# Second MoE of a two-layer block: slots gather rows of x from DRAM by an inverse permutation made on the chip and store their sums straight to the output

## The reference, cut to what matters

```python
def _L1_ffn_ref(hidden_states, router_w, gate_w, up_w, down_w):
    x = hidden_states.reshape(-1, hidden_shape[-1])
    route = jax.nn.sigmoid(x @ router_w)
    max_ind = jnp.argmax(route, axis=1)
    max_prob = jnp.take_along_axis(route, max_ind[:, None], axis=1)
    out = jnp.zeros_like(x)
    for e in range(num_experts):
        mask = (max_ind == e)[:, None]
        h = jax.nn.silu(x @ gate_w[e]) * (x @ up_w[e])
        out = out + jnp.where(mask, h @ down_w[e], 0.0)
    out = out * max_prob
    return out.reshape(hidden_shape)
...
x = x + _L1_xattn_ref(_layernorm(x, axis=-1), ctx_2048, mask_BxS2_bk0)
x = x + _L1_ffn_ref(_layernorm(x, axis=-1), L1_ffn_router_w, L1_ffn_gate_w, L1_ffn_up_w, L1_ffn_down_w)
```

## Time and profile before

| what | us |
|---|---|
| runs shown (3) | 3142.78 to 3145.83, median 3144.97 |
| the profiled execution's own time | 3145.72 |
| its span, first to last instruction | 3143.9 |
| PE, DVE, ACT, POOL busy | 2881.0, 2166.2, 2036.6, 1594.0 |
| granted TensorE clock, mean | 0.964 |

### The profile page before, as it was taken

The page is one execution under the profiler, slowest core; times in us unless marked ns, Lnnn a source line. Parts: engine busy times, 40 slices in busy tenths (PEclk is TensorE's granted clock), DMA queues, the critical chain, the costliest instruction groups (busy, mean ns, idle before and its releaser), DMA issues. The chain is left out here.

```text
span 3143.9 us, 61785 instructions
## 1 busy us (share of the span) xinstructions
PE 2881.0 (92%) x18699; PEld 2447.6 (78%) x18700; DVE 2166.2 (69%) x4564; ACT 2036.6 (65%) x5192; POOL 1594.0 (51%) x2073
## 2 busy tenths in 40 slices
PE   6886999899999999999999999999999977699495
PEld 4665888688888888888888888888888854488363
DVE  7995444577777777777777777777777768766232
ACT  5664666577777777777777777777777557565121
POOL 6993333355555555555555555555555344564201
PEclk9998999899999999999999999999999979899598
DMA  4335666611111111111101101101100020442512
GB/s 134 117 115 172 202 205 204 205 48 40 45 46 49 37 45 52 40 39 52 46 33 52 46 33 52 45 33 52 46 33 33 11 74 1 137 148 65 194 45 79
DMA packets 253176, 244.07 MB, mean 78 GB/s; under 512 B 11768, under 2 KB 233472, under 8 KB 252928
## 3 DMA queue, kind: packets, MB, share of 16 engines
q1 hardware_dynamic: 237248, 223.15, 21.7%
q10 hardware_dynamic: 14144, 13.63, 1.5%
q0 software_dynamic: 1536, 4.20, 0.4%
HBM read 151.03 MB, written 89.92 MB: 77 GB/s over the span
## 5 line engine op out<-in xcount | busy, mean ns | idle before, releaser
L911 ACT ACTIVATE pt_hi<-ps_t 128x512 fp32r<-128x512 f32 (+2 forms) x1024 | 569.9, 557 | 415.2 <-PE ps_t L1156 411.8
L983 DVE TENSOR_REDUCE piece_max<-ps_s 128x1 f32<-128x512 f32 (+2 forms) x1024 | 631.5, 622 | 258.7 <-PE ps_s L1143 231.0
L1009 DVE TENSOR_TENSOR pt_lo<-ps_t,pt_hi 128x512 fp32r<-128x512 f32 (+2 forms) x1024 | 656.3, 641 | 200.3 <-ACT pt_hi L911 183.9
L1083 POOL TENSOR_SCALAR prob<-prob,inv_sum 128x512 f32<-128x512 f32 (+2 forms) x1024 | 636.6, 641 | 270.9 <-DVE inv_sum L999 270.9
L899 ACT ACTIVATE prob<-ps_s,neg_max 128x512 f32<-128x512 f32 (+2 forms) x1024 | 648.8, 634 | 89.3 <-DVE neg_max L990 72.3
L1176 PE MATMUL ps_o<-pt_hi,v_hi 128*128 128x256 f32 (+1 forms) x1856 | 595.8, 321 | 0.0
L1156 PE MATMUL ps_t<-ident,prob 128*128 128x128 f32 (+1 forms) x3712 | 572.1, 272 | 1.4 <-DVE pt_lo L1009 1.3
L1178 PE MATMUL ps_o<-pt_hi,v_lo 128*128 128x256 f32 (+1 forms) x1856 | 523.6, 282 | 0.0
L1177 PE MATMUL ps_o<-pt_lo,v_hi 128*128 128x256 f32 (+1 forms) x1856 | 522.3, 281 | 0.0
L1156 PEld LDWEIGHTS ps_t<-ident,prob 128*128 128x128 f32 (+1 forms) x3712 | 456.7, 140 | 59.8 <-issue 1.7
L1138 PE MATMUL ps_s<-k_hi,q_hi 128*128 128x512 f32 (+2 forms) x1024 | 404.3, 395 | 34.8 <-ACT prob L899 19.8
(11 more groups left out here) (247 smaller groups left out, 5579.5 us busy)
## 6 DMA issues: line engine op xcount, KB each, us to landing
v_scratch<-v_out SPq DMA_DIRECT2D x120, 256.0 KB, 2.5
raw_k<-k_scratch SPq DMA_DIRECT2D x32, 960.0 KB, 5.5
raw_v<-v_scratch SPq DMA_DIRECT2D x32, 960.0 KB, 4.7
k_scratch<-k_out SPq DMA_DIRECT2D x104, 256.0 KB, 2.6
q_scratch<-out_t SPq DMA_DIRECT2D x64, 256.0 KB, 2.6
raw_q<-q_scratch SPq DMA_DIRECT2D x32, 512.0 KB, 3.4
c_raw<-in_ctx_t ACTq DMA_DIRECT2D x52, 256.0 KB, 2.8
raw_t<-in_ctx_t SPq DMA_DIRECT2D x24, 512.0 KB, 4.0
```

The lines of the kernel that those rows point to most:

```text
L911: nc.scalar.activation(pt_hi[keys, k % RING, cols], ps_t[keys, k % 2, cols], ACT.Copy).then_inc(hi_done, 1)
L983: nc.vector.tensor_reduce(piece_max[:, n % 2, p:p + 1], ps_s[:, p, lo - p * PC:hi - p * PC], AX.X, ALU.max).then_inc(max_ready, 1)
L1009: nc.vector.tensor_tensor(pt_lo[keys, k % RING, cols], ps_t[keys, k % 2, cols], pt_hi[keys, k % RING, cols].bitcast(F32), ALU.subtract).th ...
L1083: nc.gpsimd.tensor_scalar(prob[:, n % PB, lo:hi], prob[:, n % PB, lo:hi], inv_sum[:, n % PB:n % PB + 1], 1.0, ALU.mult, ALU.mult).then_inc ...
```

## The change

It keeps no sorted copy of xn and no y in DRAM. ACT stores each tile of x to `x_rows` in DRAM during memory_attention, two tiles behind. The routing takes each token's slot and lane from `place` and makes the inverse permutation by matmuls: `in_lane` (is this token's lane n?) turned against `facts` (token number, mean, rstd and probability, in the column of the token's slot), which leaves in `fact` for each lane and slot the token's four numbers, and from them the row to read and the row to write; a lane with no token reads row 0 and writes beyond the output, where the bounds check drops it. A slot gathers its rows of x by an indirect DMA on POOL, into a ring of four; DVE normalises them, and at the end multiplies y by the probability, adds the gathered x (`finish`) and POOL stores the sum to the output rows. The loops over slots are written out in full. The diff, its declarations and the arguments that only carry names left out; in `turn_x`, `hidden`, `output` only names, waits and the loops change, and ACT's copy of y goes:

```diff
-                sp.wait_ge(zeros_ready, 1)
-                sp.dma_start(sorted_dram.rearrange("(s p) d -> p s d", p=P), zeros[:, :].unsqueeze(1).to_broadcast([P, ESLOTS, D])).then_inc(zeroed, 16)
-                sp.wait_ge(zeroed, 16)
-                nc.gpsimd.memset(zeros[:, :], 0.0).then_inc(zeros_ready, 1)
...
+                def store_rows(i, u):
+
+                    at = i * UB + u
+                    act.wait_ge(x_added, at + 1)
+                    act.sem_inc(store_begun, 1)
+                    act.dma_start(x_rows[bass.ds(at * P, P), :], x_sb[:, bass.ds(at, 1), :].rearrange("p a n -> p (a n)")).then_inc(rows_written, 16)
...
+                            if s == 3 and u >= 2:
+                                store_rows(i, u - 2)
+                            elif s == 3 and positive(i):
+                                store_rows(i - 1, u + 2)
...
+                for u in range(2, UB):
+                    store_rows(LAST, u)
...
+                dve.wait_ge(tokens_made, 1)
+                for n, src in enumerate((token[:, :], mean_var[:, :, 0], rstd[:, :])):
+                    nc.vector.tensor_copy(own[:, :, n], src).then_inc(own_set, 1)
...
-                nc.vector.tensor_copy(max_prob[:, :], best[:, :, 0]).then_inc(prob_copied, 1)
+                nc.vector.tensor_copy(own[:, :, 3], best[:, :, 0]).then_inc(own_set, 1)
...
-                nc.vector.tensor_reduce(place_f[:, :], own_row[:, :, :], AX.X, ALU.add).then_inc(places, 1)
+                nc.vector.tensor_reduce(place[:, :], own_row[:, :, :], AX.X, ALU.add).then_inc(places, 1)
+
                 dve.wait_ge(places, 1)
-                nc.vector.tensor_copy(place[:, :], place_f[:, :]).then_inc(place_ready, 1)
+                nc.vector.tensor_scalar(slot_part[:, :], place[:, :], 1.0 / P, (P - 1) / (2 * P), ALU.mult, ALU.subtract).then_inc(slot_parts, 1)
+                dve.wait_ge(slot_parts, 1)
+                nc.vector.tensor_scalar(slot_int[:, :], slot_part[:, :], TO_INT, None, ALU.add).then_inc(slot_rounded, 1)
+                dve.wait_ge(slot_rounded, 1)
+                nc.vector.tensor_scalar(slot[:, :], slot_int[:, :], TO_INT, None, ALU.subtract).then_inc(slot_ready, 1)
+                dve.wait_ge(slot_ready, 1)
+                nc.vector.scalar_tensor_tensor(lane[:, :], slot[:, :], -float(P), place[:, :], ALU.mult, ALU.add).then_inc(lanes, 1)
+                nc.vector.tensor_tensor(in_slot[:, :, :], iota[:, 0:ESLOTS].unsqueeze(1).to_broadcast([P, NT, ESLOTS]),
+                                        slot[:, :].unsqueeze(2).to_broadcast([P, NT, ESLOTS]), ALU.is_equal).then_inc(in_slots, 1)
+                dve.wait_ge(in_slots, 1)
+                dve.wait_ge(own_set, FACTS)
+                nc.vector.tensor_tensor(facts[:, :, :, :], in_slot[:, :, :].unsqueeze(2).to_broadcast([P, NT, FACTS, ESLOTS]),
+                                        own[:, :, :].unsqueeze(3).to_broadcast([P, NT, FACTS, ESLOTS]), ALU.mult).then_inc(facts_ready, 1)
+                dve.wait_ge(lanes, 1)
+                for part in range(NORM_PARTS):
+                    tiles = slice(part * NORM_TILES, (part + 1) * NORM_TILES)
+                    nc.vector.tensor_tensor(in_lane[:, tiles, :], iota[:, :].unsqueeze(1).to_broadcast([P, NORM_TILES, P]),
+                                            lane[:, tiles].unsqueeze(2).to_broadcast([P, NORM_TILES, P]), ALU.is_equal).then_inc(in_lanes, 1)
 
...
+
+                dve.wait_ge(held, 1)
+                nc.vector.tensor_copy(fact[:, :, :], ps_f[:, :].rearrange("p (n s) -> p n s", n=FACTS)).then_inc(fact_ready, 1)
+                dve.wait_ge(fact_ready, 1)
+                nc.vector.tensor_scalar(read_at[:, :], fact[:, 0, :], 1.0, 0.0, ALU.subtract, ALU.max).then_inc(at_ready, 1)
+                nc.vector.tensor_scalar(beyond[:, :], fact[:, 0, :], 0.0, float(2 * TOK), ALU.is_equal, ALU.mult).then_inc(beyond_ready, 1)
+                dve.wait_ge(beyond_ready, 1)
+                nc.vector.tensor_tensor(holds[:, :], beyond[:, :], fact[:, 0, :], ALU.add).then_inc(holds_ready, 1)
+                dve.wait_ge(holds_ready, 1)
+                nc.vector.tensor_scalar(write_at[:, :], holds[:, :], 1.0, None, ALU.subtract).then_inc(at_ready, 1)
                 dve.wait_ge(table_ready, 1)
-                dve.wait_ge(prob_copied, 1)
+                dve.wait_ge(at_ready, 2)
...
+                pe.wait_ge(facts_ready, 1)
+                for t in range(NT):
+                    if t % NORM_TILES == 0:
+                        pe.wait_ge(in_lanes, t // NORM_TILES + 1)
+                    last = nc.tensor.matmul(ps_f[:, :], in_lane[:, t, :], facts[:, t, :, :].rearrange("p n s -> p (n s)"), start=t == 0, stop=t == NT - 1)
+                last.then_inc(held, 1)
...
+                nc.gpsimd.iota(token[:, :], [[P, NT]], base=1, channel_multiplier=1, allow_small_or_imprecise_dtypes=True).then_inc(tokens_made, 1)
                 for part in range(NORM_PARTS):
                     norm_rstd(nc, pool, mean_var, rstd, half, norm, part)
-                pool.wait_ge(xn_ready, NT)
-                pool.wait_ge(place_ready, 1)
-                for t in range(NT):
-                    nc.gpsimd.indirect_dma_start(sorted_dram, bass.IndirectOffsetOnAxis(ap=place[:, t:t + 1], axis=0), xn[:, t, :], None).then_inc(scattered, 16)
-                pool.wait_ge(scattered, 16 * NT)
...
+    RING = 4
+    LEAD = RING
-        xs = sb("xs7", [P, 2, D])
+        xg = sb("xg7", [P, RING, D])
+        xn = sb("xn7", [P, 2, D])
-        y = sb("y7", [P, 2, D])
-        back = sb("back7", [P, NT, D])
+        made = sb("made7", [P, RING, D])
...
-                def load(s, j, n):
-
-                    if positive(n):
-                        sp.wait_ge(xt_ready, s - 1)
-                        sp.sem_inc(io_begun, 1)
-                    sp.dma_start(xs[:, j, :], sorted_dram[bass.ds(s * P, P), :]).then_inc(xs_loaded[j], 16)
-
-                def step(s, j):
-                    if exists(s + 3):
-                        load(s + 3, 1 - j, 1)
-                    sp.wait_ge(y_copied, s + 1)
-                    sp.sem_inc(io_begun, 1)
-                    sp.dma_start(y_dram[bass.ds(s * P, P), :], y[:, j, :]).then_inc(y_written[j], 16)
-
-                load(0, 0, 0)
-                load(1, 1, 0)
-                load(2, 0, 1)
-                all_slots(sp, step)
-                for q in range(4):
-                    sp.wait_ge(x_added, (q + 1) * Q)
-                    sp.dma_start(out_dram[:, q * Q:(q + 1) * Q, :], x_sb[:, q * Q:(q + 1) * Q, :]).then_inc(out_written, 16)
-                sp.wait_ge(out_written, 16 * 4)
...
+            @block.gpsimd
+            def _(pool):
+                def gather(s):
+                    nc.gpsimd.indirect_dma_start(xg[:, s % RING, :], None, x_rows,
+                                                 bass.IndirectOffsetOnAxis(ap=read_at[:, s:s + 1], axis=0)).then_inc(gathered[s % RING], 16)
+
+                pool.wait_ge(rows_written[0], rows_written[1])
+                for s in range(LEAD):
+                    gather(s)
+                for s in range(ESLOTS):
+                    pool.wait_ge(made_ready, s + 1)
+                    nc.gpsimd.indirect_dma_start(out_rows, bass.IndirectOffsetOnAxis(ap=write_at[:, s:s + 1], axis=0), made[:, s % RING, :], None,
+                                                 bounds_check=TOK - 1, oob_is_err=False).then_inc(written[s % RING], 16)
+                    if s + LEAD < ESLOTS:
+                        gather(s + LEAD)
+                for j in range(RING):
+                    pool.wait_ge(written[j], 16 * ((ESLOTS + RING - 1 - j) // RING))
...
-                    act.wait_ge(y_done, s + 1)
-                    if positive(s - 1):
-                        act.wait_ge(y_written[j], 16 * (s // 2))
-                        act.sem_inc(io_begun, 1)
-                    nc.scalar.activation(y[:, j, :], ps_y[:, j, 0:D], ACT.Copy).then_inc(y_copied, 1)
...
+                def normalise(s):
+                    dve.wait_ge(gathered[s % RING], 16 * (s // RING + 1))
+                    if s >= 2:
+                        dve.wait_ge(xt_ready, s - 1)
+                    nc.vector.tensor_scalar(xn[:, s % 2, :], xg[:, s % RING, :], fact[:, 1, s:s + 1], fact[:, 2, s:s + 1],
+                                            ALU.subtract, ALU.mult).then_inc(xn_ready, 1)
+
+                def finish(s):
+
+                    dve.wait_ge(y_done, s + 1)
+                    if s >= RING:
+                        dve.wait_ge(written[s % RING], 16 * (s // RING))
+                    nc.vector.scalar_tensor_tensor(made[:, s % RING, :], ps_y[:, s % 2, 0:D], fact[:, 3, s:s + 1], xg[:, s % RING, :],
+                                                   ALU.mult, ALU.add).then_inc(made_ready, 1)
+
...
+                    if s + 2 < ESLOTS:
+                        normalise(s + 2)
                     dve.wait_ge(ht_ready, s + 1)
-                    if positive(s):
```

(62 more changed lines are left out.)

130 lines of the change are left out of this document (54 added, 76 removed).

## The result

The changed kernel takes **3124.14 us** (median of 4 runs, 3122.39 to 3126.03), the kernel before 3143.88 beside it (4 runs, 3140.10 to 3145.83): ratio 0.9939, 95% interval 0.9927 to 0.9950. It is faster, by 19.7 us, where 36.4 were forecast (3108.6), and the time lies 0.1 us beyond the end of the range. The profiled execution took 3123.67 us, its span is 3121.9.

What follows compares the result with a forecast made beforehand. TensorE, busy 92% of the span, was taken as the bound, with gains only where it stands still. Head -11.4, stage before +0.5, tail -25.5 and loop nothing sum to -36.4 us: 3144.97 becomes 3108.6, range 3103 to 3124.

Steps and rivals of the forecast that it cites:

- What bounds it: Whole kernel: TensorE is busy for 92% of the span, so a gain can only come from where it stands still.
- Head, -11.4: From the slots' places to a slot's first transpose: 2960.1 instead of 2971.5, 11.4 us earlier, as scatters and slot loads go.
- the first gather "at 2956.9": Head: first gather at 2956.9, one block boundary of 0.88 us behind DVE's last step at 2956.0.
- The stage before, +0.5: memory_attention: 15 of ACT's stores cost nothing; the last holds up the block's end, 0.5 us later.
- The loop, 5.73 against 5.82: Slot loop: the new store-gather-normalise-ht-finish ring turns in 5.73 us against 5.82 a slot, so it just fits.
- its formula for a dear turn: Slot loop: a turn up to 5.97 us costs nothing; beyond it the price is 19 x (turn - 5.82) - 2.8.
- The reason given for the low start: Loop: the first scatter's 0.96 us wait was DVE shutting POOL out; behind `finish` DVE idles, so 0.27 holds.
- The tail, -25.5: Behind the last ps_y: finish, store, landing, drain of 1.36 and end give 3118.4 instead of 3143.9, 25.5 us less.
- the ring sets the pace: Rival, slot loop: landings of 3.3 to 3.9 us make the turn 6.33 to 6.93, time 3115.5 to 3127; chance 0.24.
- The dear bounds-checked store: Rival, loop: lane-dropping store dear, kernel slower from 2.5 us more in one DMA; 3162 at 4.0; chance of slower 0.03.
- The clock: Rival, head: the 16 new matmuls raise TensorE's clock to 2.4 GHz, 3.4 and 1.9 us less, 3103.3; chance 0.04.
- as summed: Whole kernel: the time falls within 3 us of the summed forecast of 3108.6; chance 0.60.

Runs made afterwards that it cites:

- run 11: The kernel before, with only ACT's 16 stores of x in memory_attention added, which nobody reads: 3143.49 us, ratio 1.0002.
- run 8: The changed kernel with gather ahead of store, as in run 2, and the first four gathers issued in the routing's block: 3114.14 us.
- run 12: As run 9, with one spare gather of 128 rows that nobody reads, issued by POOL in its idle time of the routing: 3106.54 us.
- run 7: The changed kernel with the gathers replaced by SP's plain loads of successive rows (wrong rows summed); POOL keeps the 23 stores: 3106.37 us.
- run 5: The changed kernel with the store's bound in a register set once ahead of the loop: 3113.46 us.
- run 2: The changed kernel with gather(s+4) put ahead of the store of slot s on POOL, ring of four kept: 3111.56 us.
- run 9: The changed kernel with gather ahead of store, the bound in a register set once, and a POOL drain behind slot 19's store: 3107.64 us.

## Why the prediction was wrong, by its own steps

- **What bounds it**: right. The head, the tail and nothing else had anything to give; the loop was the risk.
- **Head, -11.4**: measured -9.4 to the first ps_g. The DVE and TensorE steps came out as summed: from `place` to the end of `write_at` 11.88 us for 11.64, ps_f 7.10 for 6.9 at the granted clock of 0.50. The step that failed is the first gather "at 2956.9", 0.88 behind DVE's end, taken from SP's start in a block: POOL came 2.01 behind it (2953.08 to 2955.09), 0.8 of it POOL's start behind SP's end of the boundary. The gather of 1.23 us, the program's first, added 0.3, and the way from the first transpose to ps_g 0.4.
- **The stage before, +0.5**: right, measured +0.6 in the traces of the changed kernel and of run 11. That the other fifteen stores cost nothing holds to within what the runs tell: up to 3.5 us by run 11, about 1 us by the length of the stage.
- **The loop, 5.73 against 5.82**: this is the step that failed, worth 13.2 of the 18.1 us between forecast and sum (-36.4 and -18.3). The mechanism was right, link by link, and so was its formula for a dear turn. Wrong was one term, POOL's start: 0.84, not 0.27. I read the low bound from a gather and gave it to a store; between them stood the register instruction of the bounds check. No row of before shows it; in the code only the constant bound points to it, which the store has and the gather has not. With 0.84 the turn is 6.30, and 19 x 0.48 - 2.8 gives 6.3 us. Store and gap, 1.33 for 1.27, add 1.1. The rest are the longer landings, 5.9 us over 2.8 summed over the slots: 1.6 in slot 6, most of the others in slots with lanes that read row 0. I named both bounds (0.96, and 896 lanes on row 0) and then took the low half of both. With all high the terms named make 7.90, not 7.94; no chance hung on that.
- **The reason given for the low start** fell. I laid the 0.96 us of the first scatter to DVE being busy, by the Trainium skill (SBUF — State Buffer, "Who interferes with whom"). The changed kernel's store starts 0.88 behind the first `made` (2975.83 to 2976.71), with DVE idle until silu at 2977.10, and 0.84 behind the one at 3041.32, with silu and hid running: DVE's work made no difference. Nor does it idle over 1 us behind `finish`, as I wrote: once the ring binds, silu follows at once (3041.24). The earlier trace rows spoke against the reading already: the scatter starts at 2945.52, while the cast of L2242 still runs, and of the four ops that I laid the wait to only the last two, 0.18 us each, are a tensor_scalar and a cast. That does not test the rule: silu and hid are tensor_tensor ops with one input in PSUM, not the kinds that it names. What delayed the first scatter is not settled. It was the program's first DMA by index, 1.25 us long, and others in that place were as late and as long: 0.94 late and 1.23 long in run 8, 0.95 and 1.23 in run 12 (the spare gather). In run 7 it was a store, 0.97 late and 1.24 long with DVE idle, where its later stores started 0.80 late and took 0.97.
- **The tail, -25.5**: measured -22.7. Two terms were mis-sized: POOL's start, 0.80 for 0.27 (the same register instruction; run 5's tail is 0.50 shorter), and the drain, 3.82 for 1.36. I carried the drain of 16 DMAs over to 46 as if it were fixed. The landing of the last store was 2.1 for 2.4.
- **The rivals**: the one that came true is "the ring sets the pace", at 0.24. Its range of turns, 5.97 to 7.2, held the measured ones, but it was priced by the landing alone with the start left low. The dear bounds-checked store was half right in kind and far off in size: 0.56 us in its start, 0.03 in itself, against the 2.5 it needed. The clock stayed at 0.50 (1.2 GHz) through the new fp32 matmuls (7.04 us busy of 8.00) and on to 2965. The Trainium skill (TensorE: Matmul & The Clock Gate, Part 1) lets sustained activity release the throttle; in this stretch, as in the router's, the trace disagrees.
- **The range**: 3103 to 3124 and 3124.14. With a step that rests on 0.24 us of margin, and three of its links priced by other instructions, 0.60 for "as summed" was too much; that case and the ring's should have changed places.
- **Of the 36.4 us**: 19.7 came at once; run 2 gives 12.6 more by exchanging two statements, run 9 another 3.9. Run 12, at 3106.5, is the fastest of those that gather, though not told apart from run 9; all three are faster than either kernel.

## What to carry to other kernels

Where a new wait closes a ring with a margin of a few tenths of a microsecond, price every link from the very instruction that will stand there, its register instructions too, and count it as bounding until shown otherwise; the remedy here was order, not speed: issue what the ring waits for ahead of what nobody waits for. Set the bound of a bounds-checked DMA once, in a register ahead of the waits. A queue of DMAs by index is paid again at the next drain, so drain it where its engine idles.

## What the runs showed of the hardware that I had not expected

- A constant bound makes a store by index start 0.84 us behind its releaser instead of 0.28, if the store is the first behind the wait; behind a gather it starts after 0.30 either way. The check itself costs 0.03 us.
- POOL's drain, once all has landed, takes 0.05 us + 0.082 us for each DMA by index since the last drain (1, 3, 16, 23, 42 and 46 DMAs: 0.14, 0.29, 1.36, 1.94, 3.48, 3.82 us).
- A gather with lanes that all read row 0 lands up to 0.8 us later than one of distinct rows (3.6 against 2.8 in the last three slots).
- The program's first DMA by index takes POOL 1.23 to 1.25 us, later gathers mostly 0.95 to 0.98, stores 0.97 to 1.02. In four kernels whose first one waited for DVE it also started 0.94 to 0.97 us late (before, runs 7, 8 and 12; in run 7 a store with a constant bound, whose later ones started 0.80 late).
